# A second z buffer, an earlier z rounding, and the second layer's bias on another engine, in the tiles behind the last chunk

## The reference

```python
x = x + relu(adj @ (item_feat @ W_item.T + b_item) + layernorm(x) @ W_user.T + b_user)   # adj: 10000 x 10000
z = layernorm(x)
probs = softmax(z @ gate_w + gate_b)                    # 8 experts
top2_vals, top2_idx = top_k(probs, 2)
for e in range(8):
    h = gelu(z @ W1[e] + b1[e])                         # 128 -> 256
    out += cw[:, e, None] * (h @ W2[e] + b2[e])         # 256 -> 128; cw is top2_vals, 0 elsewhere
x = x + out
```

## Time and profile before

| | |
|---|---|
| median of 3 runs | 1482.03 us (1476.95 to 1483.57) |
| profiled run, its own time | 1476.4 us |
| its span | 1474.6 us |
| busy: PE, DVE, ACT, POOL | 1416.1, 1244.7, 1086.2, 735.8 us |
| mean granted clock of PE | 0.993 |

### The profile page before, as it was taken

How to read it: one execution, slowest core, us unless ns; L and a number is a source line. 1 busy time by engine, 2 the same in 40 slices (tenths; PEclk the granted TensorE clock), 3 DMA queues, 4 the chain that set the end, 5 groups by cost and what they waited for, 6 DMA issues and landing times.

```text
span 1474.6 us, 20357 instructions
## 1 busy us (share of the span) xinstructions
PE 1416.1 (96%) x6617; PEld 1158.1 (79%) x6617; DVE 1244.7 (84%) x1772; ACT 1086.2 (74%) x1153; POOL 735.8 (50%) x425
## 2 busy tenths in 40 slices
PE   6999999999999999999999989999999999987778
PEld 5888888888888888888888778888888778876557
DVE  4889889889899898898898888988989889885567
ACT  4777767767767777777677687878778787875566
POOL 1004443433533542543444427778666778655781
PEclk9999999999999999999999999999999999999999
DMA  9999999999999999999999999999999989953497
GB/s 332 336 345 377 380 384 384 383 380 370 381 378 361 389 379 365 387 375 378 382 371 380 372 381 331 317 340 319 323 335 326 319 314 347 348 199 105 118 210 149
DMA packets 128811, 492.11 MB, mean 334 GB/s; under 512 B 27094, under 2 KB 32726, under 8 KB 127554
## 3 DMA queue, kind: packets, MB, share of 16 engines
q1 hardware_dynamic: 116322, 458.52, 84.2%
q0 software_dynamic: 12384, 32.30, 7.7%
HBM read 457.59 MB, written 42.59 MB: 339 GB/s over the span
## 4 chain that ended last, share of the span: by engine, by line
PE 83%; DVE 4%; issue 4%; ACT 3%; DMA 2%; SPq 1%; another core or an unknown queue 1%; ACTq 0%; DVEq 0%
PE p_agg L492 23%; PE p_agg L487 22%; PE p_agg L488 22%; DVE s_a_lo L939 2%; PE p_hid L573 2%; PE p_hid L575 2%; PE p_hid L574 2%; PE p_tp L564 1%; PE p_y L589 1%; PE p_agg L503 1%; PE p_y L591 1%; PE p_y L590 1%; PE p_hid L469 1%; PE p_y L599 1%; PE p_small L531 1%
## 5 line engine op out<-in xcount | busy, mean ns | idle before, releaser
L939 DVE TENSOR_TENSOR s_a_lo<-s_raw,s_a_hi 128x1500 fp32r<-128x1500 f32 x520 | 879.8, 1716 | 98.0 <-PE p_agg L492 57.1
L720 ACT ACTIVATE s_a_hi<-s_raw 128x1500 fp32r<-128x1500 f32 x520 | 748.7, 1454 | 201.8 <-PE p_agg L492 187.7
L487 PE MATMUL p_agg<-s_a_hi,s_h_hi 128*128 128x500 f32 x1560 | 622.8, 399 | 2.9 <-ACT s_a_hi L720 2.8
L488 PE MATMUL p_agg<-s_a_hi,s_h_lo 128*128 128x500 f32 x1560 | 605.8, 388 | 0.0
L492 PE MATMUL p_agg<-s_a_lo,s_h_hi 128*128 128x500 f32 x1560 | 443.4, 392 | 8.5 <-DVE s_a_lo L939 6.1
L1373 POOL DMA_INDIRECT zs<-s_rows,s_idx x144 | 242.9, 1687 | 273.4 <-DVE s_idx L1097 221.5
L492 PEld LDWEIGHTS p_agg<-s_a_lo,s_h_hi 128*128 128x128 f32 x1560 | 287.1, 188 | 87.0 <-DVE s_a_lo L939 25.3
L487 PEld LDWEIGHTS p_agg<-s_a_hi,s_h_hi 128*128 128x128 f32 x1560 | 293.9, 188 | 62.5 <-ACT s_a_hi L720 4.2
L488 PEld LDWEIGHTS p_agg<-s_a_hi,s_h_lo 128*128 128x128 f32 x1560 | 294.0, 188 | 58.1 <-issue 3.5
L1382 POOL DMA_INDIRECT rr<-s_ysb,s_dests x152 | 235.1, 1547 | 133.4 <-DVE s_ysb L1181 94.2
L1349 POOL TENSOR_TENSOR s_gt<-s_ebase,s_gt 125x32 f32<-125x32 f32 x20 | 128.5, 6426 | 65.8 <-DVE s_gt L1023 60.2
(11 more groups left out here) (207 smaller groups left out, 1252.5 us busy)
## 6 DMA issues: line engine op xcount, KB each, us to landing
s_raw<-adj SPq DMA_DIRECT2D x520, 750.0 KB
s_wraw<-w SPq DMA_DIRECT2D x58, 256.0 KB
s_zt<-zs SPq DMA_DIRECT2D x50, 264.0 KB
out_s<-rr POOLq DMA_DIRECT2D x12, 512.0 KB
s_xtok<-x_tok SPq DMA_DIRECT2D x20, 256.0 KB
s_xt<-x_t SPq DMA_DIRECT2D x20, 250.0 KB
zs<-s_early SPq DMA_DIRECT2D x18, 264.0 KB, 9.0
out_s<-s_x1s SPq DMA_DIRECT2D x18, 256.0 KB
```

The costliest lines, as they stand in the source:

```text
L487: mm(o, h_hi[:, k * D:(k + 1) * D], hi, start=(k == 0), stop=False)
L488: mm(o, h_lo[:, k * D:(k + 1) * D], hi, start=False, stop=False)
L720: fn(a_hi[:, n % HIS, :], raw[:, n % RAW, :], ACT.Copy).then_inc(hi_made, 1)
L939: tt(a_lo[:, n % LOS, :], raw[:, n % RAW, :], a_hi[:, n % HIS, :].bitcast(F32), ALU.subtract)\
```

## The change

In the tiles whose number is above `IN_STREAM` = 38, the rounded z and its rest go into two buffers each, taken from the finished stream's `a_hi` and `a_lo`, so that `z_round(k)` waits for the first layer of tile k - 2 in place of k - 1; the dense part's `dzh`, `dzl` move to other columns of the same tiles. On ACT, from step 520 on, `z_round` stands ahead of `gelu`. The bias of the second layer of tiles 38 to 49 is added by DVE, between `g_rest` and `y_out`, with the same waits; tile 37's stays on ACT, at the front of step 520. Tile 37's `y_turn`, `y_out` and `send` move from step 520 to 521. On POOL the variance power moves from step 522 to 521, where it stands ahead of `send(37)`.

```diff
--- before.py
+++ after.py
@@ -66,6 +66,11 @@
 BIAS = 6
 XR = 16
 
+def lag(n):
+
+    return min(n + LAG, max(n, NCH))
+
+
 
 FILL_AT = [(hi + 1) * CH for lo, hi in GROUPS]
 FIRST_ZT = [(hi + 1) * CH + 10 for lo, hi in GROUPS]
@@ -77,17 +82,12 @@
 DENSE0 = NCH + TAIL_TILES
 W1_AT += [NCH + i for i in range(TAIL_TILES + ND)]
 W2_AT = [w + (3 if w < NCH else 1) for w in W1_AT[:NT]]
-YT_AT = [w + (2 if w < NCH else 1) for w in W2_AT]
+YT_AT = [w + (2 if lag(w) < NCH else 3 if w < NCH else 1) for w in W2_AT]
 ZT_AT = [w - (3 if w < NCH else 2) for w in W1_AT[:NT]]
 SPLIT_AT = [w - (1 if o < NT else 2) for o, w in enumerate(W1_AT)]
 W_LOAD = [0, 0] + [w + 5 for w in W1_AT[:NT]]
 ZT_LOAD = [0, 0] + [max(W1_AT[k - 2] + 5, FIRST_ZT[k >= NTG[0]]) for k in range(2, NT)]
 LAST = DENSE0 + ND + 5
-
-
-def lag(n):
-
-    return min(n + LAG, max(n, NCH))
 
 
 GELU_AT, EVAC_AT, YOUT_AT = ([lag(n) for n in at] for at in (W1_AT[:NT], W2_AT, YT_AT))
@@ -257,11 +257,17 @@
         def dgl(d):
             return h_hi[:, (3 + d % 3) * 2 * UB:(4 + d % 3) * 2 * UB]
 
+        def zhi(k):
+            return a_hi[:, k % 2, 0:T] if k > IN_STREAM else zh[:, :]
+
+        def zlo(k):
+            return a_lo[:, k % 2, 0:T] if k > IN_STREAM else zl[:, :]
+
         def dzh(q):
-            return a_hi[:, q % 2, 0:UB]
+            return a_hi[:, q % 2, T:T + UB]
 
         def dzl(q):
-            return a_lo[:, q % 2, 0:UB]
+            return a_lo[:, q % 2, T:T + UB]
 
         def dy(q):
             return agg[0] if q == S + 1 else y[0]
@@ -577,7 +583,7 @@
 
             def tile_w1(k):
                 pe.wait_ge(zl_made, k + 1)
-                first_layer(k, T, zh[:, :], zl[:, :])
+                first_layer(k, T, zhi(k), zlo(k))
 
             def tile_w2(k):
                 pe.wait_ge(gl_made, k + 1)
@@ -784,11 +790,14 @@
 
             def z_round(k):
                 act.wait_ge(turned, k + 1)
-                if k >= 1:
+                if k > IN_STREAM:
+                    act.wait_ge(chunk_used, NCH)
+                    act.wait_ge(hid_ready, k - 1)
+                elif k >= 1:
                     act.wait_ge(hid_ready, k)
                 else:
                     act.wait_ge(b2_split, 1)
-                fn(zh[:, :], tp[:, :], ACT.Copy).then_inc(zh_made, 1)
+                fn(zhi(k), tp[:, :], ACT.Copy).then_inc(zh_made, 1)
 
             def gelu(k):
                 act.wait_ge(hid_ready, k + 1)
@@ -838,22 +847,23 @@
                 fn(dgh(d), dg(d), ACT.Copy).then_inc(gh_made, 1)
 
             def items(n):
+                if n >= NCH:
+                    for k in range(NT):
+                        if EVAC_AT[k] == n and W2_AT[k] < n:
+                            y_evac(k)
+                    for k in range(NT):
+                        if ZR_AT[k] == n:
+                            z_round(k)
                 for k in range(NT):
                     if GELU_AT[k] == n:
                         gelu(k)
                 if n >= NCH:
-                    for k in range(NT):
-                        if ZR_AT[k] == n:
-                            z_round(k)
                     for o in range(NT + 2):
                         if SPLIT_AT[o] == n:
                             w_round(o)
                     for k in range(NT):
                         if GELU_AT[k] == n:
                             g_round(k)
-                    for k in range(NT):
-                        if EVAC_AT[k] == n:
-                            y_evac(k)
                     return
                 for k in range(NT):
                     if EVAC_AT[k] == n:
@@ -1153,7 +1163,7 @@
 
             def z_rest(k):
                 dve.wait_ge(zh_made, k + 1)
-                tt(zl[:, :], tp[:, :], zh[:, :].bitcast(F32), ALU.subtract).then_inc(zl_made, 1)
+                tt(zlo(k), tp[:, :], zhi(k).bitcast(F32), ALU.subtract).then_inc(zl_made, 1)
 
             def ext(k):
                 dve.wait_ge(zt_loaded[k % 2], 16 * (k // 2 + 1))
@@ -1170,6 +1180,11 @@
             def g_rest(k):
                 dve.wait_ge(gh_made, k + 1)
                 tt(gl[:, :], g[:, :], gh[:, :].bitcast(F32), ALU.subtract).then_inc(gl_made, 1)
+
+            def y_evac(k):
+                dve.wait_ge(w2_done, k + 1)
+                dve.wait_ge(y_turned, k)
+                nc.vector.tensor_scalar(yt[:, :], y[0][:, :], bias[:, k % BIAS, 2:3], None, ALU.add).then_inc(yt_made, 1)
 
             def y_out(k):
                 dve.wait_ge(y_turned, k + 1)
@@ -1212,6 +1227,9 @@
                     for k in range(NT):
                         if GELU_AT[k] == n:
                             g_rest(k)
+                    for k in range(NT):
+                        if EVAC_AT[k] == n and W2_AT[k] == n:
+                            y_evac(k)
                     for k in range(NT):
                         if YOUT_AT[k] == n:
                             y_out(k)
@@ -1415,7 +1433,7 @@
                     pool.wait_ge(fill_set, 1)
                     gp.tensor_scalar(fill[:, :, D + 1], dest0[:, :], float(DUMP + PADS * T), None, ALU.add)\
                         .then_inc(fill_set, 1)
-                if n == NCH + 2:
+                if n == NCH + 1:
                     power_of_rs(BLOCKS)
                 if n == NCH + 5:
                     power(BLOCKS - 1)
```

## The result

The changed kernel takes 1474.63 us in the median of 20 runs (1471.81 to 1482.28), the kernel before 1478.92 in 20 runs beside it (1476.34 to 1483.57): a ratio of 0.9977, 95% interval [0.9967, 0.9986]. That is a gain of 3.4 us by the ratio (2.1 to 4.9), where 8.0 was forecast. The time itself came near the forecast of 1474.0 only because the three runs shown first were 3 us above what the kernel before takes in twenty. One execution of a later version (e7_adds_early) took 2811 us and is left out of its ratio.

What follows compares the result with a forecast made beforehand. PE was taken to set the pace up to 1334.7 us and PE's side the end, POOL's close behind. Terms 4.8 + 2.7 + 1.1 - 0.6 = 8.0 took the 1482.0 us median to 1474.0, range 1469.4 to 1481.0.

Steps and rivals of the forecast that it cites:

- Tile 37's bias add first, start of tile 39: Step 520: PE's 3.88 us stall goes, tile 39's first layer starts at 1339.3 instead of 1344.14, gain 4.8 us.
- New loop: Tiles 39 to 49: beat falls from 4.83 to 4.22 us, gain 6.1, less 3.4 for last block's gating: 2.7.
- Dense weights: ACT's 4.9 us of waits for dense weights, asked for sooner beside POOL's transfers: costed at -0.6 us (0 to -5).
- PE's side sets the end: End of the span: PE's side, closing with DVE's last add at 1471.98 and 2.6 us after it, ends last.
- a margin of 4.7 us: End of the kernel before: POOL's side ready at 1469.9, that much ahead of PE's side.
- POOL's cap: End of the kernel: POOL's side, ending at 1466.0 after the change, allows at most 8.6 us of gain.
- POOL's side is 3.9 sooner: POOL's tail: tile 38's scatters 1.8 us sooner and the 2.13 us pause gone, end 1469.9 to 1466.0.
- B: Rival: DVE's bias add holds POOL's scatters up, 7.2 us later; gain 1.4, time 1480.6 us; chance 0.07.
- C: Rival: two z buffers bridge part of the 11.4 us remote stalls, POOL caps gain at 8.6; 1473.4 us; chance 0.12.
- D: Rival: remote stalls hit DVE's bias-add waits and block PE; three of 3 us give 1483.0 us; chance 0.07.
- E: Rival: only the start gains, beat stays at 4.83 us; gain 4.8, time 1477.2 us; chance 0.15.
- A: Rival: half the gain, DVE becomes the pacer, gating exposed and add near 1.2 us; gain 3.9, 1478.1 us; chance 0.19.

Runs made afterwards that it cites:

- e7_adds_early: Changed kernel with POOL's variance power back in step 522 and the 512 KB transfers moved forward by up to six steps: ratio 0.9956, 1470.48 us.
- e6: Kernel before without POOL's last transfer, the accumulating add of second-choice rows of blocks 12 to 17: ratio 0.9928, 1466.19 us.
- e5: Changed kernel without POOL's last transfer, the accumulating add of second-choice rows of blocks 12 to 17: ratio 0.9908, 1463.01 us.
- e3: Kernel before with only tile 37's edits and the variance power's move to step 521: ratio 0.9989, 1476.05 us.
- e2: Changed kernel with POOL's variance power back in step 522, behind tile 37's send: ratio 0.995, 1470.86 us.
- e10: Changed kernel, power back in step 522, DVE's two small copies right behind Gelu's rest, bias add ahead of that rest: ratio 0.997, 1470.17 us.
- e11: Changed kernel with the bias of tiles 38 to 49 back on ACT and the variance power back in step 522: ratio 0.9952, 1468.23 us.
- e1: Changed kernel with the bias of tiles 38 to 49 added by ACT again, all else as changed: ratio 0.9961, 1472.05 us.
- e4: Kernel before with only the bias of tiles 38 to 49 moved to DVE: ratio 1.0000, 1477.22 us.

## Why the prediction was right, and where not

*Tile 37's bias add first, start of tile 39.* Right: 4.5 sooner against 4.8 (1339.67 for 1344.14).

*New loop.* Wrong in size, and the total hid it. DVE's last add came 7.9 sooner (8.0 forecast), but e6 and e5, which run the code of before and of after up to the transfer left out, have no remote wait and make the cleaner pair. There that add ends at 1459.8 and at 1454.4: 5.4 sooner. Tile 39's first layer starts 4.9 sooner (1339.62 for 1344.56), the ten beats from tile 39 to tile 49 take 49.5 for 50.0, a gain of 0.6 where 2.7 was forecast, and the rest gives -0.1 where 0.5 was. The other 2.4 of the 7.9 are lateness that differs between executions: against its clean mate the profile of before is late by 12.1 on PE's side and that of after by 9.7. The sum held this at nothing, so the agreement of the total is luck.

The term that was mis-sized is the beat of 4.22. The bias add itself took 0.74 for 0.75. But `gh` is one buffer, so rounding Gelu's output waits for the second layer of the tile before, and the sum has no such wait. PE, ACT, DVE, DVE and PE again, in the kernel after:

```profile
1356.64 0.47 PE L595 MATMUL p_y<-s_gh,s_wt 128*128 128x512 f32 x1 [1.06 <-DVE s_yt L1187]
1358.38 1.06 ACT L814 ACTIVATE s_gh<-s_g 128x1024 fp32r<-128x1024 f32 x1 [0.66 <-PE p_y L597]
1359.47 1.23 DVE L1182 TENSOR_TENSOR s_gl<-s_g,s_gh 128x1024 fp32r<-128x1024 f32 x1 [1.03 <-issue]
1360.61 0.74 DVE L1187 TENSOR_SCALAR s_yt<-p_y,s_bias 128x512 f32<-128x512 f32 x1
1361.50 0.47 PE L595 MATMUL p_y<-s_gh,s_wt 128*128 128x512 f32 x1 [0.96 <-DVE s_yt L1187]
```

Second layer to rounding 1.74, to Gelu's rest 1.09, to the bias add 1.14, to the next second layer 0.89: 4.86 for one tile, as much as the old beat. Where the bias add is not between Gelu's rest and the second layer this loop is shorter, and the beats show it. Ten beats, in traces without remote waits: 49.9 in e3 (one z buffer, bias on ACT), 49.4 in e2 and 49.5 in e5 (the new loops, bias on DVE behind Gelu's rest), 45.6 in e10 (ahead of it), 44.8 in e11 (on ACT, seven of the ten at 4.27 to 4.29). So the forecast beat is that of the new z buffers with the bias add left on ACT. Waits in the kernel after:

```profile
POOL out_s L1382 <- DMA out_s<-rr: 18.5, 2, 14.7
PEld p_y L595 <- DVE s_gl L1182: 16.1, 10, 3.9
POOL rr L1400 <- issue: 15.9, 53, 0.3
PE p_y L595 <- DVE s_yt L1187: 11.8, 9, 3.5
```

Dense weights cost ACT 6.4 against 4.9, 1.5 more for 0.6 forecast.

*"PE's side sets the end", "a margin of 4.7 us".* This is the step that failed. It was read off one execution, and e6 shows an execution of the same code with POOL's side 7.6 us later (1450.74 for 1443.19) and PE's 12 sooner. From POOL's last power to the last pair of 512 KB transfers it took 65.1 us in the profile of before and 71.3 in e6. Two things make nearly all of the 6.2: long scatters (in all over 0.96 us: 4.1 and 7.8) and the wait for the transfers of the first rank (1.33 and 3.68), 3.7 + 2.35. So the chance set on POOL's cap was too low, and a faster PE could bring only what POOL's side gained. That the kernel got only 3.4 of the 8.0 is due to this step, whatever PE's side gained.

*"POOL's side is 3.9 sooner".* Against the shown profile it is 4.5 later, by steps: the power and the pause of 2.13 were to bring it to its last power 3.9 sooner, and it came at 1374.26 for 1374.21; long scatters took 4.8 us ahead of that point for 1.2 before, and the start was 0.5 late (1348.27 for the 1347.8 assumed). Behind it, 1.4 more of long scatters and 2.5 more of waiting for the first rank; less 1.7 of waiting for scatters to land; and 2.3 more for the first big transfer (14.66 for 12.34): 0.05 + 1.4 + 2.5 - 1.7 + 2.3 = 4.5. Against e6, the fairer mate, the big transfer is issued 5.3 sooner. The 3.4 measured is of the size of this, and only by chance that of the forecast 3.9.

*The unpriced part.* The power's move puts tile 37's scatters behind a wait of 9.02 us. The forecast listed what is queued behind it, but compared it only with the old order under the old loop. e2 gives the likely price: 0.27% between the two ratios, some 4 us, with intervals that touch. Between e1 and e11, with the bias on ACT, it is 0.09%, within the intervals, and e10 is no clear gain either; so the size stays open.

*Rivals.* B, scatters held by the bias add: the symptom came (lengths of 1.4 to 2.1), the cause did not (e10's rows, the count, and e3, where the bias add is on ACT and scatters are held all the same). The row that spoke against B, "keep their pitch while DVE subtracts out of SBUF", was misread: the scatter at 1358.63 had begun 0.12 before the subtraction at 1358.75, and what has begun is not held. The Trainium skill ("SBUF — State Buffer", "Who interferes with whom") also says that a DVE instruction with two SBUF inputs contends with a GpSimd instruction that reads SBUF. By that clause, left out of the prediction, the subtractions hold scatters and the bias add does not, if a scatter counts as such an instruction (it takes its offsets from SBUF): the traces agree, 228 of 228. C's mechanism, that POOL's side caps the gain, is the nearest, with a cap of 3 to 5 and not 8.6. D did not come: no bias add of DVE waited on remote in the kernel after, and in e4 one did, for 0.5 us. Of PE's side, E is nearest to the clean pair: the start gains, and the mean beat is 4.95, by the `gh` loop that E did not name. A's sign came in part, 16.1 us of PE's weight loads in ten waits for `s_gl`, but DVE had holes in these very beats (1.03 ahead of 1359.47), so it was not the pacer.

## What to carry to other kernels

When two engines' sides end within a few microseconds of each other, one profiled execution does not tell which sets the end: take the last piece off one side and see whether the time moves, before working on the other. When a wait is moved ahead of work in a queue, price it under the new schedule, against leaving it where it is. When an instruction is put between two others of a queue, look for every loop that it then lies in, those through a buffer that exists only once above all. A queue of scatters on POOL should be counted by how often it starts under a subtraction that has both sources in SBUF.

## What the runs showed of the hardware

A POOL indirect scatter of 0.96 us that starts over 0.1 us into a DVE subtraction with both sources in SBUF ends 0.75 to 1.0 us after that subtraction, so up to 2.1 us long; started up to 0.1 us after the subtraction's start it may get through or may be held; begun under a PSUM-source subtraction, product or bias add alone, none took over 1.1. POOL's four scatters (4 times 1.26) and the tile beat drift against each other, so the loss depends on where they meet: over the tail the scatters ran over 0.96 us by 5.3 us in the profile of before and by 9.9 in e6, which is the same code there, and by 5.3 to 11.3 over all fourteen traces.

An accumulating transfer of 1536 KB from DRAM to DRAM kept POOL waiting 9.5 to 14.7 us for its landing, and a store of 250 KB issued beside it in the kernel after took 11.2; with two halves of 768 KB issued together it could go on 10.6 and 14.2 us after the first issue.

The waits put down to "remote" (15.6 us in before, 6.3 to 9.9 in three others, none in the remaining ten) come and go between executions of the same code (15.6 in before and none in e6, 7.0 in after and none in e5); what causes them stays open.
